# First attention's scores in two 64-row halves of the operand tiles, the pieces by key and the halves by query taken in turns

## The reference, cut to what matters

```python
xn = _layernorm(x)                                 # x: (2, 1024, 128)
# first attention: 16 heads of 8, causal, rotary q and k
q, k, v = split(xn @ qkv_w.T + qkv_b)
scores = einsum('bhqd,bhkd->bhqk', rope(q), rope(k)) / sqrt(8)
attn = softmax(where(causal, -max, scores))
a = einsum('bhqk,bhkd->bhqd', attn, v) @ out_w.T + out_b
# second part: 6 nodes in a row, each an attention of 8 heads of 16, not causal
o = softmax((q @ wq) @ (k @ wk).T / 4) @ (v @ wv) @ wo
nodes[c] = act_w[c] * o + q
return x + a + _layernorm(nodes[5]) * ln_g + ln_b
```

## Time and profile before

| what | us |
|---|---|
| median of 3 runs | 1426.18 (1425.83 to 1427.39) |
| the profiled execution | 1423.05 |
| its span, first to last instruction | 1421.3 |
| PE / DVE / ACT / POOL busy | 1380.5 / 1263.0 / 1139.5 / 449.8 |
| mean granted clock of TensorE | 0.991 |

### The profile page before, as it was taken

One profiled execution on the slowest core, in us unless ns is written; L12 is line 12 of the kernel. 1 busy time (PEld: TensorE's weight loads), 2 busy tenths in 40 slices (PEclk: granted clock), 3 DMA queues, 4 the chain that ended last, 5 costly groups with the idle time before them and its releaser, 6 DMA issues.

```text
span 1421.3 us, 60282 instructions
## 1 busy us (share of the span) xinstructions
PE 1380.5 (97%) x26216; PEld 935.3 (66%) x26216; DVE 1263.0 (89%) x1587; ACT 1139.5 (80%) x2133; POOL 449.8 (32%) x936
## 2 busy tenths in 40 slices
PE   6899999999999999999999999999999999999995
PEld 4467777656667666676676766766667666667652
DVE  8889999999989989899899898988989989989895
ACT  3378887688878878888788887887888878878784
POOL 5141115324422433233423332234233432330210
PEclk9899999999999999999999999999999999999998
DMA  8131112343232422333323323233233332321211
GB/s 253 47 116 60 51 59 98 119 142 119 81 127 70 132 97 77 102 109 107 104 78 114 107 74 121 83 123 107 69 101 107 101 107 80 127 98 56 76 38 40
DMA packets 115668, 137.68 MB, mean 97 GB/s; under 512 B 14972, under 2 KB 90109, under 8 KB 115277
## 3 DMA queue, kind: packets, MB, share of 16 engines
q1 hardware_dynamic: 115405, 133.83, 28.7%
HBM read 64.63 MB, written 61.98 MB: 89 GB/s over the span
## 4 chain that ended last, share of the span: by engine, by line
PE 88%; DMA 4%; DVE 3%; SPq 2%; ACT 1%; POOL 1%; issue 1%; ACTq 0%; POOLq 0%; DVEq 0%
PE s L1069 53%; PE cps L1163 26%; PE misc L1069 7%; DMA qs<-mrows 2%; DVE neg_max L971 1%; SPq L431 1%; PE misc L1064 1%; ACT probs L784 1%; DMA dram_raw_b<-csb 1%; PE s L1064 0%; DVE s L967 0%; POOL parts L601 0%; POOL ks L596 0%; POOL full L614 0%; SPq L500 0%
## 5 line engine op out<-in xcount | busy, mean ns | idle before, releaser
L784 ACT ACTIVATE probs<-s 128x512 f32<-128x512 f32 x1792 | 1059.2, 599 | 227.4 <-PE s L1069 166.8
L971 DVE TENSOR_REDUCE neg_max<-s 128x1 f32<-128x1024 f32 x768 | 936.5, 1222 | 62.0 <-PE s L1069 9.1
L1069 PE MATMUL s<-qs,ks 99*32 99x512 bf16 (+2 forms) x7680 | 808.4, 370 | 7.1 <-DMA qs<-mrows 5.1
L1069 PE MATMUL s<-ks,qs 96*32 96x512 bf16 (+2 forms) x7680 | 606.5, 369 | 6.3 <-DMA ks<-dram_qk_a 2.7
L1163 PE MATMUL cps<-probs,vs 128*32 128x256 f32 (+1 forms) x7552 | 591.4, 368 | 0.6 <-ACT probs L784 0.6
L1069 PEld LDWEIGHTS s<-qs,ks 99*32 99x32 bf16 x7680 | 235.8, 94 | 240.6 <-ACT probs L784 96.7
L1163 PEld LDWEIGHTS cps<-probs,vs 128*32 128x32 f32 x7552 | 316.4, 110 | 76.3 <-issue 17.0
L1069 PEld LDWEIGHTS s<-ks,qs 96*32 96x32 bf16 x7680 | 292.5, 97 | 88.6 <-issue 24.5
L633 POOL TENSOR_TENSOR mparts<-neg_max,zeros 128x8 bf16<-128x8 f32 x128 | 26.0, 203 | 796.0 <-DVE neg_max L971 654.3
L967 DVE CUSTOM_DVE_ANT_0 s<-s,mask_q 128x1024 f32<-128x1024 f32 (+7 forms) x256 | 187.8, 785 | 23.5 <-PE s L1069 14.8
L706 POOL TENSOR_TENSOR parts<-full,zeros 128x512 bf16<-128x512 f32 x48 | 61.4, 1280 | 52.2 <-DVE full L949 52.2
(11 more groups left out here) (134 smaller groups left out, 607.6 us busy)
## 6 DMA issues: line engine op xcount, KB each, us to landing
dram_qk_b<-parts SPq DMA_DIRECT2D x48, 384.0 KB, 3.2
qs<-dram_qk_b SPq DMA_DIRECT2D x96, 192.0 KB
ks<-dram_qk_b SPq DMA_DIRECT2D x96, 192.0 KB
dram_qk_b<-parts SPq DMA_DIRECT2D x48, 256.0 KB, 3.2
dram_raw_b<-csb SPq DMA_DIRECT2D x93, 128.0 KB, 4.3
dram_qk_b<-parts SPq DMA_DIRECT2D x48, 128.0 KB, 3.2
vsrc<-srcT SPq DMA_DIRECT2D x12, 512.0 KB, 3.1
ctx_b<-dram_raw_b SPq DMA_DIRECT2D x44, 128.0 KB
```

Of the source, the lines that this page charges most:

```text
L784: nc.scalar.activation(buf[:, lo:hi], s2[bank][:, 0:hi - lo], ACT.Exp, scale=scale).then_inc(exp_done, 1)
L971: last = ve.tensor_reduce(peak, scores, AX.X, ALU.max, negate=True)
L1069: last = te.matmul(dst[c0:c0 + STRIP, :], lhsT[:, c0:c0 + STRIP], rhs, start=start, stop=stop, tile_position=(0, c0))
```

## The change

Unit k's A operands no longer stand in `qs` and `ks` but in two new tiles `qa`, and in `ka`, which are two halves of `ctx_b` (not in use until B). Each holds two units: 48 rows of data and 3 rows of maxima or ones, from partition 0 (units 0 and 1 of four) or from partition 64 (units 2 and 3). A's matmuls read 48 or 51 rows and are placed on the upper or the lower 64 rows of the array; since by key and by query are two units apart, they stand on different halves. B's are as before. The mask product takes 64 of its 128 rows; where the strip's diagonal lies in the other half it takes `mask_far`, a mask moved by 64. The order of an A turn becomes: first piece by key, first half by query, second piece by key, second half by query, context. VectorE zeroes only `vs` and fills `ka` with ones; GpSimd writes the ones of `ks` before the power instead of at the end, and makes two more masks.

```diff
+        def first_row(which, k):
+
+            return HALF_ROWS * (k % RING // 2) if which == "A" else 0
...
+        def operands(which, k):
+
+            return (qa[k % 2], ka[k % 2]) if which == "A" else (qs[k % RING], ks[k % RING])
...
+            for s in range(RING):
+                pool.wait_ge(pool_const, 8 + s)
+                pl.memset(ks[s][MROW:128, :], 1.0).then_inc(pool_const, 1)
...
             for s in range(RING):
-                for ring in (qs[s][:, :], ks[s][:, :], vs[s][:, :, :]):
-                    ve.memset(ring, 0.0).then_inc(dve_const, 1)
+                ve.memset(vs[s][:, :, :], 0.0).then_inc(dve_const, 1)
+            for n in range(2):
+                ve.memset(ka[n][:, :], 1.0).then_inc(dve_const, 1)
...
-            def mm_strips(dst, lhsT, rhs, start=True, stop=True):
+            def mm_strips(dst, lhsT, rhs, start=True, stop=True, row=0):
 
                 for c0 in range(0, 128, STRIP):
                     last = te.matmul(dst[c0:c0 + STRIP, :], lhsT[:, c0:c0 + STRIP], rhs, start=start, stop=stop,
-                                     tile_position=(0, c0))
+                                     tile_position=(row, c0))
...
+            def mask_strips(dst, row):
+
+                rows = slice(row, row + HALF_ROWS)
+                for c0 in range(0, 128, STRIP):
+                    here = c0 // HALF_ROWS == row // HALF_ROWS
+                    at, mask = (c0, mask_k) if here else ((c0 + HALF_ROWS) % 128, mask_far[row // HALF_ROWS])
+                    last = te.matmul(dst[c0:c0 + STRIP, :], ident_h[rows, at:at + STRIP], mask[rows, :],
+                                     start=False, stop=True, tile_position=(row, c0))
+                return last
...
-                            for t, at, end in query_tiles(kind[0], i):
-                                for lo, hi in pieces(kind[0], i):
-                                    lo, hi = max(lo, at), min(hi, end)
+                            chunks = pieces(kind[0], i)
+                            for c0, c1 in chunks:
+                                for t, at, end in query_tiles(kind[0], i):
+                                    lo, hi = max(c0, at), min(c1, end)
                                     if lo >= hi:
                                         continue
-                                    last = mm_strips(s1[n % 2][:, lo:hi], q[0:KROW, t * 128:(t + 1) * 128],
-                                              ky[0:KROW, lo - at:hi - at])
+                                    last = mm_strips(s1[n % 2][:, lo:hi], q[rows, t * 128:(t + 1) * 128],
+                                                     ky[rows, lo - at:hi - at], row=row)
+                                if rest and c0 == 0 and len(chunks) > 1 and kind[0] == "A":
+                                    score_piece(kind, r, k, j, 1)
+                                    rest = []
                             last.then_inc(s1_ready, 1)
```

More of the change, by code:

```diff
@@ L27 @@
 KALL = KROW + 3
+ROWS_A = 6 * DA
+HALF_ROWS = 64
 STRIP = 32
@@ L273, in dual_attention_kernel @@
         mask_k = sb("mask_k", [128, 128], BF16)
+        mask_far = [sb(f"mask_far{n}", [128, 128], BF16) for n in range(2)]
+        qa = [sb(f"qa{n}", [128, S], BF16) for n in range(2)]
         ones_row = sb("ones_row", [1, 128])
@@ L297, in dual_attention_kernel @@
         exps = {"B": probs, "A": probs + [rec_b]}
+        ka = [ctx_b[:, n * CH:(n + 1) * CH].bitcast(BF16) for n in range(2)]
         s1 = [pb(f"s1_{n}", [128, S]) for n in range(2)]
@@ L429, in load_unit @@
                     need(sp, written, 4 * 3 * 16 * PREPS.after(kind, r))
-                for op, dst in ((0, qs[slot]), (1, ks[slot])):
-                    sp.dma_start(dst[0:6 * dims, :],
+                for op, dst in enumerate(operands(which, k)):
+                    sp.dma_start(dst[data_rows(which, k), :],
                                  qk_dram[which][op, :, bass.ds(row * dims, dims), :]
                                  ).then_inc(qk_in[slot], 16)
-            sp.wait_ge(dve_const, 3 * RING)
+            sp.wait_ge(dve_const, RING + 2)
             sp.wait_ge(pool_const, N_CONST)
@@ L567, in _ @@
             pl.memset(mask_q[:, :], 0.0).then_inc(pool_const, 1)
-            pl.memset(mask_k[:, :], 0.0).then_inc(pool_const, 1)
-            pool.wait_ge(pool_const, 3)
+            for mask in (mask_k, *mask_far):
+                pl.memset(mask[:, :], 0.0).then_inc(pool_const, 1)
+            pool.wait_ge(pool_const, 5)
             pl.affine_select(out=ident[:, :], in_=ident[:, :], pattern=[[-1, 128]], compare_op=ALU.not_equal,
@@ L590, in _ @@
                              ).then_inc(pool_const, 1)
[L591 removed]
+            pool.wait_ge(dve_const, RING)
             for s in range(RING):
                 pl.memset(vs[s][:, :, LROW:LROW + 1], 1.0).then_inc(pool_const, 1)
[L594 to L596 removed]
             pool.wait_ge(pool_const, N_CONST)
@@ L1277, in score_piece @@
                 which = kind_at(kind, k, 2)
-                q, ky = qs[(k - 2) % RING], ks[(k - 2) % RING]
+                q, ky = operands(which, k - 2)
+                rows, row = score_rows(which, k - 2), first_row(which, k - 2)
                 lo, hi = pieces(which, j)[n]
@@ L1287, in score_piece @@
                     diagonal = which == "A" and first == at
-                    last = mm_strips(bank[:, first - lo:end - lo], ky[0:KALL, t * 128:(t + 1) * 128],
-                                     q[0:KALL, q0 + first - at:q0 + end - at], stop=not diagonal)
+                    last = mm_strips(bank[:, first - lo:end - lo], ky[rows, t * 128:(t + 1) * 128],
+                                     q[rows, q0 + first - at:q0 + end - at], stop=not diagonal, row=row)
                     if diagonal:
-                        last = mm_strips(bank[:, at - lo:at - lo + 128], ident_h[:, :], mask_k[:, :],
-                                         start=False)
+                        last = mask_strips(bank[:, at - lo:at - lo + 128], row)
                 last.then_inc(s2_ready, 1)
@@ L1309, in phase @@
                         if kind != "T":
-                            q, ky = qs[k % RING], ks[k % RING]
+                            q, ky = operands(kind[0], k)
+                            rows, row = data_rows(kind[0], k), first_row(kind[0], k)
                             if i == 0:
```

26 lines of the change are left out of this document (19 added, 7 removed).

## The result

| | before | after |
|---|---|---|
| median of 8 runs each, same comparison | 1426.01 (1422.76 to 1428.61) | 1431.51 (1424.77 to 1434.07) |
| ratio of after to before | | 1.0035 (95%: 1.0021 to 1.0050) |
| the profiled execution | 1423.05 | 1424.77 |
| its span | 1421.3 | 1423.0 |

The forecast was 1417.6 us, faster. The kernel became 5.5 us slower. One thing has to be seen first: the profiled execution of after is the fastest of its eight, with a mean granted clock of 0.987. The other seven took 1431.0 to 1434.1 us, at 0.977 to 0.981. So the profile shows the rarer course, and the experiments have to show the common one. (Of the experiments, one slow execution of e3, of 1483.28 us, and one of e11, of 4392.74 us, are left out of medians and ratios.)

A forecast was written before the change was run, and what follows sets the result against it. TensorE's scores and contexts were taken to set A's pace. A's units (-9.1 us), B0 (+1.0) and the start (-0.5) summed to -8.6 us, on the median 1426.18 giving 1417.6 us; range 1410 to 1432.

The forecast's parts named there:

- A0's first two steps: Two of the five A0 units with rotary matmuls, each taken to gain 0.4 us.
- B0 +1.0: Last two A units among B scores: 36 changes, 3.4 us if bare, partly covered by VectorE, so 1.0 us lost.
- Overlap across rows, and no strict order: In A, by-key and by-query halves fully overlap, hiding 1.93 us a unit; rivals: no overlap 0.08, strict order 0.07.
- A change costs 0.095: In A and B0, each switch between half and all rows costs 0.095 us, ten a unit in A; bounds 0 and 0.27.
- Dear changes: Rival: changes between half and all rows also wait for results, up to 0.27 us each, 1450 us; chance 0.20.
- The ring of 6.22: An A unit's cycle of by-key pieces through ScalarE and TensorE's stream: 6.18 us, taken as 6.22 against 6.50.
- 20 plain steps x 0.28 = 5.6: Twenty A units without rotary work or projections gain 0.28 us each, 5.6 us together.
- this chain at 5.6 us a unit: SyncE's chain from operand issue to the maxima's landing, with a context's store, ends at 5.6 us and binds only below.
- Waits for ScalarE take the place of TensorE's stream: In A, TensorE's own stream falls to 5.3 us a unit, but then it waits for exponentials.
- AZ 0.3 a step: Five AZ units with a projection gain 0.3 us each, half of 7.35 to about 6.75, together 1.5 us.
- A0 0.4 a step: Five A0 units with two rotary matmul groups gain 0.4 us each, together 2.0 us.
- The start -0.5: Less zeroing on VectorE lets the statistics begin 1.4 us sooner; 0.5 us gained, bounds 0 and -1.5.

The follow-up runs named there:

- e3: Changed kernel with all A units on the same half of the rows, so nothing can overlap: 1465.45 us, 1.0286 of the kernel before.
- e11: Changed kernel with all 128 rows in A0's first two steps only, B0's A pieces still on half rows: 1429.48 us, 1.0006 of the kernel before.
- e2: Kernel before with only the new order of a turn, operands on full rows and the old start: 1425.58 us, 1.0006 of the kernel before.
- e10: Changed kernel with all 128 rows both in A0's first two steps and for B0's A pieces, result complete: 1418.54 us, 0.9936 of the kernel before.
- e7: Kernel before with only B0's A pieces by key on half rows, those units' maxima left out: 1433.15 us, 1.0058 of the kernel before.
- e9: Changed kernel with B0's A pieces on all 128 rows, foreign rows zeroed, result complete: 1423.51 us, 0.9971 of the kernel before.
- e1: Changed kernel, nothing altered, profiled a second time: one execution, 1439.69 us.
- e4: Changed kernel with extra float32 matmuls of 512 columns before and in A0's first two steps: 1432.86 us, 1.0066 of the kernel before.
- e6: Changed kernel with both A pieces by key of a B0 turn together, 10 changes a step instead of 18: 1427.29 us, 1.0031 of the kernel before.
- e8: Changed kernel with many small bfloat16 matmuls of 128 columns before and in A0's first two steps: 1431.30 us, 1.0052 of the kernel before.
- e12: Changed kernel with the old order of a turn, whole by-query group before the second by-key piece: 1433.59 us, 1.0051 of the kernel before.
- e5: Changed kernel with B0's A pieces reading 96 rows of B's operands on full rows, two units' result left out: 1419.09 us, 0.9967 of the kernel before.

## Why the prediction was wrong

**TensorE's clock was not in the sum, and it decided the sign.** No term of it speaks of the granted clock; every duration was taken from rows at 2.4 GHz. The sum had -8.6 us. The step that failed is the pricing of A0's first two steps (-0.8) and of B0 (+1.0): both were counted from the stream, the changes and VectorE's cover, at the full clock. What the runs showed in its place:

- *A0's first two steps*, forecast -0.8 (two of five at 0.4), were +2.6, since the low clock stayed to 62.1 us in place of 48.7. That it is the half rows and not the order is shown by e2 (full rows, new order: 49.8) and e3 (half rows, no overlap: 74.3); that it is these two steps' rows by e10 and e11 (50.7 and 46.0). The rise scatters by itself: with full rows it came at 46.0 to 56.7 us in five profiles, with half rows and no filler at 62.1 to 74.3 in seven. Against e7, the one of 56.7, with 18.6 us for the two steps, the loss would be 1.4 and not 2.6. e10 is 0.35% or 5 us below e9. In their two profiles 2.1 of 4.9 us lie behind B0's third transpose, where the programs are the same, so what these rows are worth is some 3 to 5 us.
- *B0*. The step "B0 +1.0" counted 18 changes a step and how far VectorE covers them. At full clock it came to +2.3, or +2.7 with the third step, inside its bounds of 0 to 3.4. But in six of the seven profiles of changed kernels that overlap and have half rows in B0 (e1, e4, e6, e8, e11, e12; not after) the clock falls at 261 to 269 us and stays down for 14 to 34 us. e7 shows that B0's half-row pieces alone bring the loss to the kernel before (+0.58%), e5 and e9 that without them after is faster than before (0.33% and 0.29%), though it still has the late clock in A0. So it is B0 that decides the sign.

What goes before the fall is a pause in the work: TensorE waits there for the maxima on their way through DRAM. In after:

```profile
263.69 0.40 PE L1103 MATMUL s<-qa,ctx_b 51*32 51x512 bf16 x4 [1.76 <-DMA qa<-mrows]
```

and in before, at the same place of the program:

```profile
267.07 0.40 PE L1069 MATMUL s<-qs,ks 99*32 99x512 bf16 x4 [1.70 <-DMA qs<-mrows]
```

The pause is in every kernel, but its length differs, and so does what stands behind it (one profile each; a fall begins 0.1 to 2.4 us after the pause's end):

| behind the pause | pause, and how long the clock is at 1.2 GHz after it |
|---|---|
| full rows, before's program there | before 1.70, none; e2 1.76, none |
| full rows, changed kernel | e5 2.02, 3.4; e9 2.22, 3.4; e10 1.88, 3.4 |
| half rows, no overlap | e7 (before's steps) 1.42, none; e3 0.64, none |
| half rows, changed kernel with the overlap | after 1.76, none; e12 1.71, 20.5; e1 1.94, 34.1; e6 2.10, 13.7; e8 2.17, 17.1; e11 2.23, 20.5; e4 2.25, 13.7 |

So whether the clock falls goes with the length of the pause: no fall at 0.64 to 1.76, a fall at 1.88 to 2.25, e12 being the one exception. The longer pauses are all in changed kernels. How long the clock stays down goes with the rows behind: 3.4 us with full rows, 13.7 to 34.1 with half rows alternating with all rows. Whether the half-row form or the drains at the changes keep it down is not told apart. A filler in the pause, or maxima that come sooner, was not tried, so that the longer pause is what lets the clock fall is likely and not shown.

**Point by point, the rest.**

- *Overlap across rows, and no strict order*: right; starts 0.03 us apart, a by-query group ahead of the mask written before it. e3 against after gives its worth, 1.31 us a step.
- *A change costs 0.095*: right. It is 0.10 in both directions, and 0.106 by the steps of e3 and e2. The longer 0.17 at some entries is a wait for ScalarE. "Dear changes" did not come true.
- *The ring of 6.22*: right in its make-up, 0.09 too short; the plain step is 6.31. In after, by-key pieces start at 142.79 (a), 144.49 (b), 145.48 (a), 147.19 (b), 148.14 (a) and 149.09 (a). The link from a over ScalarE to b takes 1.70 and 1.71 where the sum had 1.74, TensorE's stretches 0.99, 0.95 and 0.95 where it had 0.90 three times.
- *20 plain steps x 0.28 = 5.6*: 2.5 over the 20 steps. Fourteen steps take 6.31, a gain of 0.19 in place of 0.28; the others take up to 6.97. In the longest the chain goes over SyncE's issues and the landing of the maxima. The chain of after, 118 to 132 us:

```profile
by line: PE s L1103 32.8%; DMA qa<-mrows 23.2%; PE cps L1207 19.7%; SPq L458 13.0%; ACT probs L817 4.3%; SPq L527 3.2%; issue 2.8%; PE s L1113 2.1%; PE misc L1385 0.3%; ACTq L816 0.1%
...
118.98 1.05 SPq L458
120.07 0.45 SPq L527
120.52 0.05 issue
120.57 3.24 DMA qa<-mrows
```

The prediction had this chain at 5.6 us a unit, from one landing of 2.58; in this step the landing took 3.24 and the step 6.97. Before has such steps too (7.00 us with a landing of 2.97 in its chain, and 6.77 with the 2.58 of the earlier trace rows). But its steps exceed 6.50 by 1.1 us in all over AL, those of after exceed 6.31 by 2.4.

- *Waits for ScalarE take the place of TensorE's stream*: right. The waits of after, 93 to 222 us (total, times, longest):

```profile
PEld s L1103 <- ACT probs L817: 34.2, 121, 0.4
ACT probs L817 <- PE s L1113: 13.4, 41, 1.0
```

34.2 us over 20 steps is 1.7 a step; before, the first of these rows was 3.3 us.

- *AZ 0.3 a step*: right, 0.29. *A0 0.4 a step*: right for the third to fifth (1.2 over three), wrong for the first two.
- *The start -0.5*: -0.6 in the two profiles, but the same start came 2.1 us later in e1, so it is neither shown nor refuted.

Without the clock the same terms, as measured, would be -0.6 - 2.0 - 2.5 - 1.5 + 2.7 = -3.9 us, taking A0's five steps at 0.4: faster by 0.3%. e10, almost without either trouble of the clock, is at 0.64% or -9.1 us, near the -8.6 of the sum, but that is in good part chance. It has no changes in B0, and its profiled span is only 4.4 us below that of before (1416.9 against 1421.3): the profiled execution of before is itself 3 us faster than its median, and no trace shows where the others lose them.

## What to carry to other kernels

Packing matmuls on halves of the rows pays only where two halves really run side by side, and each change between half and all rows costs 0.10 us on a full TensorE: count the changes first. Keep half-row matmuls out of the stretches where they stand alone or alternate with full-row ones, above all where the clock is still low or TensorE has just waited; they have nothing to overlap with there, and zero rows, so that they use the whole array, turned 0.35% slower into 0.64% faster. And look at the granted clock of several executions, not of the profiled one alone: here the one profile hid most of the loss.

## What was not expected of the hardware

- The granted clock does not follow busy time alone: in before it rose at 48.7 us, with TensorE busy for 10.97 of the 12 us from 38; in after, busy for 11.51 of them and 11.72 of the next 12, it rose at 62.1; in e3 it was 0.50 through 12 us that were all busy.
- The clock differs between executions of one kernel: B0's first three steps took 33.0 us in one of after and 48.1 in another (e1), a difference of 1.1% of the span.
- Where the clock fell after a pause of TensorE (1.71 to 2.25 us), it was down for 3.4 us with full rows behind the pause and for 13.7 to 34.1 with half and all rows alternating.
- Entering half rows costs as much as leaving them, 0.10 us.
